# A new order of the transfer queue around the softmax shifts, an earlier first shift, and ten matmuls without use

## The chip, the cores and the metric

The kernel runs on one core of one Trainium2 chip. The metric is the device time of one execution in microseconds (us), as the median of several runs. The engines are TensorE (PE in the profile, its weight loads PEld), VectorE (DVE), ScalarE (ACT), GpSimd (POOL) and SyncE (SP), which here only issues transfers (SPq).

## The reference

An x of 1024 tokens by 256 features goes through four residual steps. The changed code lies in the first, attention over 16 heads of 16 with low-rank additions to its four weights:

```python
def lora_linear(x, W, b, Bm, Am):
    out = jnp.einsum('bld,od->blo', x, W) + b
    upd = jnp.einsum('blr,or->blo', jnp.einsum('bld,rd->blr', x, Bm), Am)
    return out + SCALING * upd
q = _split(lora_linear(x, Wq, bq, Bq, Aq))
k = _split(lora_linear(x, Wk, bk, Bk, Ak))
v = _split(lora_linear(x, Wv, bv, Bv, Av))
scores = jnp.einsum('bhqd,bhkd->bhqk', q, k) * SCALE
attn = jax.nn.softmax(scores, axis=-1)
out = jnp.einsum('bhqk,bhkd->bhqd', attn, v)
...
return lora_linear(out, Wo, bo, Bo, Ao)
...
x = x + _L0_attn_a_ref(_layernorm(x, axis=-1), ...)
x = x + _L0_ffn_ref(_layernorm(x, axis=-1), ...)
x = x + _L0_attn_b_ref(_layernorm(x, axis=-1), ...)
x = x + _L0_ffn_ref(_layernorm(x, axis=-1), ...)
```

## The kernel before

The program is written engine by engine; each engine runs its own list in the order of the code, and semaphores tie the lists together. There are three stages.

**Setup** (to about 52 us). Layer norm, transposes, and each weight merged with its low-rank part on PE (`merged_weight`, 4 identity products and 2 short ones, each fp32 product counted twice by the profile, into one bank of PSUM, then copied to `wT` by ACT). K and Q are projected and cut into a first fp16 part and a rest. For the scores each head needs its rows packed side by side, 64 rows of keys and of queries; that packing is done by transfers alone, most of them on SP's queue (`near_keys`, `queries`, `whole_group`). The heads form four groups of four (`G = 4`, `NG = 4`). Group 0 is packed head by head, group 1 right behind it; each whole group ends with two large transfers that repeat the rows on the other 64 partitions. A head of groups 2 and 3 takes 6 transfers of SP (two halves of rows, for the keys and for each half of the queries), so a group takes 24, and then the two repeats.

**Attention**, in eight units (a group and one half of the queries; `NU = 8`). A unit is done twice over, in two passes:
- The *max pass* finds each query's largest score: `max_tile` (PE, two matmuls side by side into a pair of banks, four pairs of products a head, 16 tiles a unit) and `take_max` (DVE, one reduction over 128x1024 a tile, `mx`). The banks alternate between two pairs, so tile k waits until DVE has taken tile k-2. After 16 tiles `cut_max` splits the 16 columns of maxima into two fp16 parts (`m_parts`). `shift_rows` turns them to rows on PE, `copy_shift` (ACT) takes them to `m_rows`, and `land_shift` (SP, 8 KB) writes them into rows of the packed queries. That subtraction, "the shift", then comes with the score product itself, so no score tile of the unit may start before its shift has landed (`shift_landed`).
- The *score pass*: `score_tile` (PE, one matmul, three banks in a ring), exp (ACT), and `times_v` (PE, 4 fp32 products, counted as 8, for every 4 score tiles, summed in bank 6, `PV_BANK`), 8 of these a unit.

PE runs the score pass of unit u beside the max pass of unit u+1 in one written order, `unit`. A unit's max pass is ahead: its first 7 tiles (`LEAD`) are done in the last part of the unit before. The shift of unit u+1 is turned at step 23 of unit u (`SHIFT_AT`) and is waited for at step 32, the first score tile of unit u+1. Ahead of unit 0 there is a lead of its own, in straight code: 7 max tiles of unit 1, and among them the sums of the feed-forward weights, the merge of Wo (used only after attention), the first shift, and the first three score tiles.

SP's list around it: group 1, the shift of unit 0, group 2 whole, two bias loads to be used after attention, the shift of unit 1, group 3 whole, the shift of unit 2, and the other five shifts. ACT waits for the packing of groups 2 and 3 at the end of its units 0 and 1 together, PE for group 2 at that place and for group 3 two units later.

**The tail** (from about 207 us): the last unit's scores beside everything else, in an order written out as one table of events for all engines. The change touches nothing there.

Names for PSUM banks: `drained5` counts how often bank 5 has been read out, `filled5` how often it was filled.

## Time and profile before

| | us |
|---|---|
| median of 3 runs | 353.88 |
| lowest, highest | 352.8, 354.6 |
| the profiled execution | 356.42 |
| its span, first to last instruction | 354.6 |
| mean granted clock of TensorE in it | 0.966 |
| PE busy | 327.8 (92%) |
| DVE busy | 280.8 (79%) |
| ACT busy | 243.6 (69%) |
| POOL busy | 128.5 (36%) |

All times below are read from the profiled execution and count from the start of its span. "Busy" is the time in which an engine worked on an instruction; of PE it says less than of the others, since matmuls overlap. "Granted clock" is the share of TensorE's full 2.4 GHz; it has two levels here, 1.00 and 0.50 (1.2 GHz).

### The profile page before, as it was taken

The page shows a single profiled execution, that of the slowest core. Times are in us where ns is not written, and L with a number is a line of the kernel's source. Part 1 is how long each engine was busy: PE and PEld are TensorE (multiplying, and loading weights), DVE is VectorE, ACT ScalarE, POOL GpSimd, SP SyncE. Part 2 cuts the span into 40 slices and gives each one's busy share as a digit, 9 for nine tenths or more (in the row PEclk, how much of TensorE's full clock was granted, in tenths as well). Part 3 has the DMA queues.
Part 4 walks back from the last instruction along what each step waited for, and adds up shares of the span by engine and source line. Part 5 has one row for each costly group of instructions (what it writes and reads, how often), then busy time and mean ns, then how long its engine had stood idle before and what let it go on. Part 6 is the DMA issues. An engine that isn't in the chain of part 4 may idle for free.

```text
span 354.6 us, 5515 instructions
## 1 busy us (share of the span) xinstructions
PE 327.8 (92%) x1909; PEld 146.6 (41%) x1909; DVE 280.8 (79%) x471; ACT 243.6 (69%) x465; POOL 128.5 (36%) x133
## 2 busy tenths in 40 slices
PE   7999787999979999999999999999998979789796
PEld 2653342222212222222222235339645736347585
DVE  6456999899968999999999443527869987989764
ACT  1575113688958898988889866896579333577694
POOL 5042018999200000000005001300599949995030
PEclk9999998799989999999999999999999969989899
DMA  7927861354340000000000000000000000000011
GB/s 214 321 58 122 146 181 30 71 115 85 63 91 0 3 0 1 2 0 3 0 3 1 3 1 2 0 0 2 0 3 0 1 0 2 0 0 2 1 61 59
DMA packets 14814, 14.57 MB, mean 41 GB/s; under 512 B 4995, under 2 KB 13126, under 8 KB 14598
## 3 DMA queue, kind: packets, MB, share of 16 engines
q1 hardware_dynamic: 12358, 12.09, 15.1%
q10 hardware_dynamic: 2176, 1.64, 1.5%
q0 software_dynamic: 256, 0.52, 0.8%
q8 instruction: 15, 0.25, 0.3%
q14 instruction: 9, 0.07, 0.1%
HBM read 5.78 MB, written 1.05 MB: 19 GB/s over the span
## 4 chain that ended last, share of the span: by engine, by line
PE 61%; SPq 10%; DVE 8%; ACT 7%; POOL 5%; DMA 4%; issue 3%; ACTq 0%; DVEq 0%; POOLq 0%
PE ps L1419 14%; PE ps L1405 12%; SPq L535 8%; PE ps L1547 6%; PE ps L1559 6%; PE ps L1382 5%; DVE mx L1097 3%; POOL pbuf L750 3%; PE ps L1334 3%; PE ps L1532 3%; PE ps L1591 2%; PE ps L1364 2%; DMA parts<-pbuf 1%; DMA pack<-m_rows 1%; ACT ps L931 1%
## 5 line engine op out<-in xcount | busy, mean ns | idle before, releaser
L1097 DVE TENSOR_REDUCE mx<-ps 128x1 f32<-128x1024 f32 x128 | 150.4, 1219 | 10.2 <-PE ps L1382 9.0
L888 ACT ACTIVATE pbuf<-ps 128x512 f32<-128x512 f32 x256 | 135.8, 601 | 29.7 <-PE ps L1405 28.5
L1405 PE MATMUL ps<-pack 64*128 64x512 f16 x256 | 87.9, 387 | 3.7 <-DMA pack<-m_rows 1.9
L1419 PE MATMUL ps<-pbuf,v_slot 128*32 128x512 f32 x512 | 69.7, 618 | 1.2 <-ACT parts L873 1.2
L1405 PEld LDWEIGHTS ps<-pack 64*128 64x128 f16 x256 | 23.1, 94 | 82.2 <-ACT pbuf L888 49.3
L1382 PE MATMUL ps<-pack 64*128 64x512 f16 x128 | 49.2, 387 | 5.1 <-DVE mx L1097 4.2
L750 POOL TENSOR_TENSOR pbuf<-wT 128x1024 f32<-128x1024 f32 (+3 forms) x32 | 48.3, 1550 | 4.7 <-ACT wT L960 4.7
L1382 PE MATMUL ps<-parts,pack 64*128 64x512 f16 x128 | 50.0, 396 | 0.0
L705 POOL COPY v_slot<-v_sb 128x512 f32<-128x512 f32 x8 | 4.8, 612 | 114.2 <-PE ps L1419 92.2
L681 POOL TENSOR_TENSOR rstd<-rstd,minus_half 128x2 f32<-128x2 f32 x16 | 11.4, 715 | 72.4 <-DVE rstd L1016 72.4
L1191 DVE SCALAR_TENSOR_TENSOR pack<-ps,g_unit,pack 128x512 f16<-128x512 f32 (+1 forms) x40 | 24.7, 640 | 15.2 <-ACT pack L943 15.1
L1547 PE MATMUL ps<-v_sb,w_nat 128*128 128x512 f16 (+1 forms) x160 | 32.8, 351 | 2.4 <-DVE v_sb L1183 2.4
L1559 PE MATMUL ps<-w_nat,pack 128*128 128x256 bf16 x256 | 31.4, 273 | 0.2 <-DVE pack L1191 0.2
L931 ACT ACTIVATE ps<-ps,b_col 128x512 f32<-128x512 f32 (+1 forms) x40 | 23.4, 610 | 8.9 <-PE ps L1547 8.9
L1204 DVE TENSOR_REDUCE s_wide<-pbuf 128x64 f32<-128x1024 f32 (+3 forms) x32 | 25.4, 813 | 2.2 <-POOL pbuf L750 2.1
L1559 PEld LDWEIGHTS ps<-w_nat,pack 128*128 128x128 f16 x256 | 25.0, 98 | 4.9 <-issue 0.6
L943 ACT ACTIVATE pack<-ps,g_unit 128x512 f16<-128x512 f32 (+1 forms) x40 | 23.5, 642 | 0.2
L953 ACT ACTIVATE xn<-x_res,offset,rstd 128x256 f32<-128x256 f32 x24 | 13.1, 595 | 14.6 <-POOL offset L686 14.5
L1547 PEld LDWEIGHTS ps<-v_sb,w_nat 128*128 128x128 f16 x160 | 15.8, 102 | 16.4 <-issue 3.6
L1382 PEld LDWEIGHTS ps<-pack 64*128 64x128 f16 x128 | 11.9, 94 | 23.4 <-DVE mx L1097 12.3
L1419 PEld LDWEIGHTS ps<-pbuf,v_slot 128*32 128x32 f32 x512 | 10.5, 108 | 18.9 <-issue 18.2
L1591 PE MATMUL ps<-w_nat,xT 128*128 128x512 f32 x32 | 17.2, 664 | 0.0
(145 smaller groups left out, 392.0 us busy)
## 6 DMA issues: line engine op xcount, KB each, us to landing
w_nat<-in_L_ffn_w_dram SPq DMA_DIRECT2D x2, 1024.0 KB, 6.7
pack<-pack SPq DMA_DIRECT2D x3, 512.0 KB, 4.9
pack<-pbuf SPq DMA_DIRECT2D x20, 64.0 KB, 3.0
x_res<-in_L_attn_a_x_dram SPq DMA_DIRECT2D x4, 256.0 KB, 3.9
pack<-parts SPq DMA_DIRECT2D x16, 64.0 KB, 2.3
pack<-parts SPq DMA_DIRECT2D x32, 32.0 KB, 2.0
out_dram<-x_res SPq DMA_DIRECT2D x4, 256.0 KB, 2.1
w_nat<-in_L_attn_b_Wqkv_dram ACTq DMA_DIRECT2D x1, 768.0 KB, 4.8
```

What stands on the lines that cost most here:

```text
L535: eng.dma_start(rows[ROWS // 2 * i:ROWS // 2 * i + ROWS // 2], terms).then_inc(done, 16)
L750: pool.tensor_tensor(out, in0, in1, ALU.mult).then_inc(products, 1)
L888: act.activation(pbuf[:, c % 2, j, :], ps[:, b, :], ACT.Exp, scale=scale_reg).then_inc(drained[b], 1)
L931: act.activation(src, src, ACT.Gelu, bias=b1_col[:, f:f + 1]).then_inc(gelu_ready, 1)
L1097: dve.tensor_reduce(mx[:, par, k:k + 1], ps[:, b:b + 2, :].rearrange("p b k -> p (b k)"), AX_X, ALU.max) \
L1191: dve.scalar_tensor_tensor(out=g_lo[:, kept(r, s), f, 0:width], in0=bank(key)[:, 0:width], scalar=g_unit[:, f:f + 1], in1=g_hi[:, kept(r, ...
L1204: dve.tensor_reduce(s_raw[:, t % 2, i, 0:nj], terms, AX_X, ALU.add).then_inc(reduced, 1)
L1382: ins = pe.matmul(ps[:, b + n, :], q.rearrange("p g t -> p (g t)"), keys.rearrange("p g t -> p (g t)"), start=True, stop=True)
L1405: pe.matmul(ps[:, b, :], k_group[0:ROWS, at, j, P * c:P * c + P].rearrange("p g t -> p (g t)"), q_rows[0:ROWS, at, qh, j, :].rearrange("p ...
L1419: ins = pe.matmul(ps[32 * j:32 * j + 32, PV_BANK, :], v_slot[:, qh, c, j, :], pbuf[:, c % 2, j, :], start=(c == 0), stop=(c == TT - 1))
L1547: ins = pe.matmul(out, w1T[:, c, P * f:P * f + P], x12[:, part, c, v], start=(part == 0 and c == 0), stop=(part == 1 and c == DC - 1))
L1559: ins = pe.matmul(out, part[:, k, f, v], w2T[:, f, :], start=(f == 0 and n == 0 and i == 0), stop=(f == FC - 1 and n == 1 and i == 1))
```

## The change

Three edits, of which none changes what is computed.

1. On PE, in the lead: the weight sums stay behind max tile 0; the first shift's transpose and Wo's merge move from behind tile 0 to behind tile 1, in the opposite order. Their two banks are swapped with that (shift 5, merge 7). ACT copies the shift ahead of Wo's merged weight.
2. On PE, behind each of the lead's tiles 2 to 6: two matmuls of 128x512 bf16 on constants into bank 6, whose result is overwritten (`KEEP_UP = 2`).
3. On SP: the first head of group 2 ahead of the first shift, the other three behind it; the second shift behind group 2's repeats and ahead of the bias loads; the third shift behind three of group 3's heads, and the fourth head and the repeats behind that.

```diff
@@ setup order
-    return [("proj", 6), ("proj", 7), *(("v", t) for t in range(TT)), ("wsum",), ("wt", O_), ("shift",)]
+    return [("proj", 6), ("proj", 7), *(("v", t) for t in range(TT)), ("wsum",), ("shift",), ("wt", O_)]
@@ SP
+            sp.wait_ge(rest_ready, len(ITEMS))
+            pack_heads(2, 0, 1)
             land_shift(0, 0, 0)
-            sp.wait_ge(rest_ready, len(ITEMS))
+            pack_heads(2, 1, G - 1)
             sp.wait_ge(abs_ready, 2)
-            whole_group(2)
+            repeat_group(2)
+            land_shift(0, 1, 1)
             is_drained(sp, ("wt", O_))
             for tile, name in ((b2_all, "L0_ffn_b2"), (bout_all, "L0_attn_b_bout")):
                 sp.dma_start(tile, a[name].unsqueeze(0).broadcast_to([P, D])).then_inc(later_bias_in, 16)
-            land_shift(0, 1, 1)
-            whole_group(3)
+            pack_heads(3, 0, G - 1)
             land_shift(1, 0, 2)
+            pack_heads(3, G - 1, 1)
+            repeat_group(3)
@@ ACT
-            evacuate_weight(O_)
-            act.wait_ge(cols_in, 16)
...
             copy_shift(0)
+            evacuate_weight(O_)
+            act.wait_ge(cols_in, 16)
@@ PE
-            def keep_clock(n):
+            def keep_clock(n, b):
                 for _ in range(n):
-                    pe.matmul(ps[:, PAIR_BANKS[0], :], onesb[:, 0:P], onesb[:, :], start=True, stop=True)
+                    pe.matmul(ps[:, b, :], onesb[:, 0:P], onesb[:, :], start=True, stop=True)
...
             for k in range(LEAD):
                 max_tile(0, 1, 1, k)
                 if k == 0:
+                    weight_sums(("wsum",))
+                if k == 1:
                     pe.wait_ge(consts, 6)
-                    weight_sums(("wsum",))
+                    shift_rows(0)
                     merged_weight(("wt", O_))
-                    shift_rows(0)
+                    is_drained(pe, ("v", TT - 1))
+                if k >= LEAD - 5:
+                    keep_clock(KEEP_UP, PV_BANK)
                 if k == LEAD - 4:
                     pe.wait_ge(far_keys_packed, 16 * G)
                     pe.wait_ge(shift_landed, 16)
```

`pack_heads(g, first, n)` issues the packing transfers of n heads, `repeat_group(g)` waits for the group's packing and issues the two repeats; together they are the old `whole_group`.

PE's list in the lead, before: `abs_sum` is the weight sums, the four rows behind it are the merge and the shift's transpose, `pack`/`parts,pack` pairs are max tiles, a single `pack` is a score tile.

```order
L1358 MATMUL ps<-abs_sum,ones 128x2 [waits drained4,abs_ready,consts]
L1296 MATMUL ps<-ident,w_nat 128x128 [waits drained5,w_in3]
L1296 MATMUL ps<-ident,w_nat 128x128 x3
L1302 MATMUL ps<-aT,b_all 128x256 x2
L1396 MATMUL ps<-identh,m_parts 128x128 [waits drained7,shift_split]
L1382 MATMUL ps<-pack 128x512 [waits drained2]
L1382 MATMUL ps<-parts,pack 128x512
L1382 MATMUL ps<-pack 128x512 [waits drained0]
L1382 MATMUL ps<-parts,pack 128x512
L1382 MATMUL ps<-pack 128x512 [waits drained2]
L1382 MATMUL ps<-parts,pack 128x512
L1405 MATMUL ps<-pack 128x512 [waits drained4,shift_landed,far_keys_packed]
```

And now:

```order
L1390 MATMUL ps<-pack 128x512 [waits drained2]
L1390 MATMUL ps<-parts,pack 128x512
L1404 MATMUL ps<-identh,m_parts 128x128 [waits drained5,shift_split,consts]
L1304 MATMUL ps<-ident,w_nat 128x128 [waits drained7,w_in3]
L1304 MATMUL ps<-ident,w_nat 128x128 x3
L1310 MATMUL ps<-aT,b_all 128x256 x2
L1390 MATMUL ps<-pack 128x512 [waits drained0,drained6]
L1390 MATMUL ps<-parts,pack 128x512
L1372 MATMUL ps<-onesb 128x512 x2
L1390 MATMUL ps<-pack 128x512 [waits drained2]
L1390 MATMUL ps<-parts,pack 128x512
L1372 MATMUL ps<-onesb 128x512 x2
```

Max tile 1 and the shift's transpose stand ahead of the merge, and pairs of constant matmuls (`onesb`) stand between the tiles.

SP's list from group 1's repeats on, before (`pack<-parts` is the packing of group 2 or 3, `pack<-m_rows` a shift):

```order
L615 DMA pack<-pack 64x4096
L629 DMA pack<-m_rows 2x16x128 [waits drained7]
L535 DMA pack<-parts 32x1x1024 [waits abs_ready,rest_ready]
L535 DMA pack<-parts 32x1x1024
L535 DMA pack<-parts 32x1x512 x4
L535 DMA pack<-parts 32x1x1024 x2
...
L613 DMA parts<-pack 64x4x512 [waits group_packed2]
L615 DMA pack<-pack 64x4096
L638 DMA w_nat<-in_L_ffn_b_dram 128x256 [waits drained5]
L638 DMA w_nat<-in_L_attn_b_bout_dram 128x256
L629 DMA pack<-m_rows 2x16x128 [waits drained7]
L535 DMA pack<-parts 32x1x1024 x2
```

And now:

```order
L536 DMA pack<-parts 32x1x1024 [waits rest_ready]
L536 DMA pack<-parts 32x1x1024
L536 DMA pack<-parts 32x1x512 x4
L633 DMA pack<-m_rows 2x16x128 [waits drained5]
L536 DMA pack<-parts 32x1x1024 x2
L536 DMA pack<-parts 32x1x512 x4
...
L616 DMA parts<-pack 64x4x512 [waits group_packed2,abs_ready]
L618 DMA pack<-pack 64x4096
L633 DMA pack<-m_rows 2x16x128 [waits drained7]
L645 DMA w_nat<-in_L_ffn_b_dram 128x256 [waits drained7]
L645 DMA w_nat<-in_L_attn_b_bout_dram 128x256
```

One head's six transfers moved ahead of the first shift, and the second shift moved ahead of the two bias loads. The end of SP's list for the attention, now:

```order
L536 DMA pack<-parts 32x1x1024 x2
L536 DMA pack<-parts 32x1x512 x4
L633 DMA pack<-m_rows 2x16x128 [waits drained7]
L536 DMA pack<-parts 32x1x1024 x2
L536 DMA pack<-parts 32x1x512 x4
L616 DMA parts<-pack 64x4x512 [waits group_packed3]
L618 DMA pack<-pack 64x4096
L633 DMA pack<-m_rows 2x16x128 [waits drained7] x5
```

The third shift, which stood behind both repeats of group 3, stands ahead of its last head.

## Rows read from the trace of the kernel before

**Rows 1.** The page, 40 equal slices of the span: TensorE's granted clock, in tenths.

```profile
PEclk9999998799989999999999999999999969989899
```

**Rows 2.** Stretches: length; busy us (instructions) of PE, PEld, DVE, ACT, POOL; clock, DMA share, GB/s.

```profile
57.00:59.00 2.00, 0.95 (x6) 0.39 (x7) 2.00 (x3) 0.84 (x2) 1.84 (x2) 0.98 0.45 74
59.00:61.00 2.00, 1.89 (x6) 0.21 (x3) 2.00 (x3) 0.84 (x2) 1.91 (x2) 0.50 0.18 37
...
101.00:103.00 2.00, 0.10 (x3) 0.06 (x3) 1.27 (x2) 0.46 (x1) 0.00 (x0) 1.00 0.55 115
...
105.00:107.00 2.00, 2.00 (x13) 0.29 (x6) 0.37 (x1) 0.25 (x2) 0.51 (x1) 0.58 0.00 0
```

**Rows 3.** PE's timeline in the lead: start, us, line, operation, count, idle before and releaser.

```profile
52.59 1.14 PE L1296 MATMUL ps<-ident,w_nat 128*128 128x128 f32 x8
54.71 0.23 PE L1396 MATMUL ps<-identh,m_parts 128*128 128x128 f16 x1
54.88 0.39 PE L1382 MATMUL ps<-pack 64*128 64x512 f16 x1
...
57.66 0.37 PE L1405 MATMUL ps<-pack 64*128 64x512 f16 x1 [0.68 <-issue]
...
63.35 1.93 PE L1419 MATMUL ps<-pbuf,v_slot 128*32 128x512 f32 x8
...
66.85 1.07 PE L1419 MATMUL ps<-pbuf,v_slot 128*32 128x512 f32 x8
```

**Rows 4.** DVE's timeline over the same stretch.

```profile
53.32 0.18 DVE L1106 SCALAR_TENSOR_TENSOR m_parts<-mx,m_parts 128x16 f16<-128x16 f32 x1
...
55.31 9.14 DVE L1097 TENSOR_REDUCE mx<-ps 128x1 f32<-128x1024 f32 x8 [0.55 <-PE ps L1382]
66.10 8.40 DVE L1097 TENSOR_REDUCE mx<-ps 128x1 f32<-128x1024 f32 x7 [1.65 <-PE ps L1382]
```

**Rows 5.** The timeline of SP's transfer queue: when each was issued, and how long issuing took.

```profile
48.09 0.62 SPq L615 DMA_DIRECT2D pack<-pack  x1
55.60 0.78 SPq L629 DMA_DIRECT2D pack<-m_rows  x1
56.51 16.70 SPq L535 DMA_DIRECT2D pack<-parts  x24
...
76.71 2.04 SPq L638 DMA_DIRECT2D w_nat<-in_L_attn_b_bout_dram  x1
78.80 0.73 SPq L629 DMA_DIRECT2D pack<-m_rows  x1
79.58 16.16 SPq L535 DMA_DIRECT2D pack<-parts  x24
...
97.85 0.61 SPq L615 DMA_DIRECT2D pack<-pack  x1
98.51 0.72 SPq L629 DMA_DIRECT2D pack<-m_rows  x1
```

**Rows 6.** PE's and PEld's timeline at the first score tile of units 1 and 2.

```profile
81.15 0.11 PEld L1405 LDWEIGHTS ps<-pack 64*128 64x128 f16 x2 [0.46 <-DMA pack<-m_rows]
...
102.94 0.39 PE L1405 MATMUL ps<-pack 64*128 64x512 f16 x1 [1.90 <-DMA pack<-m_rows]
```

**Rows 7.** The shifts of units 1 to 4 turned on PE, from the timeline.

```profile
75.50 0.23 PE L1396 MATMUL ps<-identh,m_parts 128*128 128x128 f16 x1 [0.41 <-DVE m_parts L1106]
...
95.36 0.23 PE L1396 MATMUL ps<-identh,m_parts 128*128 128x128 f16 x1
...
118.73 0.23 PE L1396 MATMUL ps<-identh,m_parts 128*128 128x128 f16 x1
...
138.44 0.23 PE L1396 MATMUL ps<-identh,m_parts 128*128 128x128 f16 x1
```

**Rows 8.** Timeline behind unit 3's shift: its issue by SP; ACT's copy of unit 2's output.

```profile
119.29 0.66 SPq L629 DMA_DIRECT2D pack<-m_rows  x1
...
127.12 0.58 ACT L873 COPY parts<-ps 128x512 f32 x1
```

More of the change, by code:

```diff
@@ L73 @@
 WARM_UP = 17
+KEEP_UP = 2
 SCORE_BANKS = (4, 5, 7)
@@ L605, in _, with pack_heads @@
             sp.dma_start(q_rows[ROWS:2 * ROWS, 0, 1, :, :], q_rows[0:ROWS, 0, 1, :, :]).then_inc(second_half_repeated, 16)
-            def whole_group(g):
-                for h in range(G * g, G * g + G):
+            def pack_heads(g, first, n):
+                for h in range(G * g + first, G * g + first + n):
                     near_keys(sp, h, whole, group_packed[g])
@@ L611, in whole_group, with repeat_group @@
                         queries(sp, h, 0, qh, group_packed[g])
+            def repeat_group(g):
                 sp.wait_ge(group_packed[g], group_count(g))
@@ L616, in whole_group @@
                              q_rows[0:ROWS, g, :, :, :].rearrange("p s j t -> p (s j t)")).then_inc(group_repeated[g], 16)
-            whole_group(1)
+            pack_heads(1, 0, G)
+            repeat_group(1)
             def land_shift(g, qh, u):
@@ L1361, in _ @@
                      "v": project_v, "wsum": weight_sums, "norm2": norm_squared}
-            def keep_clock(n):
+            def keep_clock(n, b):
                 for _ in range(n):
-                    pe.matmul(ps[:, PAIR_BANKS[0], :], onesb[:, 0:P], onesb[:, :], start=True, stop=True)
+                    pe.matmul(ps[:, b, :], onesb[:, 0:P], onesb[:, :], start=True, stop=True)
             pe.wait_ge(consts, 4)
-            keep_clock(WARM_UP)
+            keep_clock(WARM_UP, PAIR_BANKS[0])
             for key in setup_order():
```

## The prediction

> **What bounds the kernel now.** First the page's slices [rows 1]: TensorE's clock is below full in slices 7 and 8 (53 to 71 us), in slice 12 (98 to 106 us) and in three slices of the tail. The change touches the first two places. The stretches narrow them down [rows 2]: the clock is 0.50 from 59 to 61 us (it fell at 58.9), PE did 0.10 us of work from 101 to 103, and behind that the clock is down again, from 103.2 until past 106. Nowhere else between 60 and 200 us is PE idle for long. So in the regular part PE sets the pace, and there is a ruler for it: the shifts, turned once a unit [rows 7], at 75.50, 95.36, 118.73 and 138.44. The last interval is 19.71 us and has neither an idle PE nor a low clock in it. The one before is 23.37, the one before that 19.86. What exceeds 19.71 is what the places of the second kind cost in all, wait and clock together: 3.66 and 0.15 us.
>
> Then the reasons. At 102.94 PE had waited 1.90 us for a transfer `pack<-m_rows` [rows 6], the shift of unit 2. ACT had its rows ready at about 95.9 (unit 3's shift, met by an idle SP, is issued 0.56 us behind its transpose [rows 7, 8]; for unit 2 that is 95.92). SP issued it at 98.51 [rows 5], because it stood behind group 3's last packing, its landing and both repeats; and it landed 4.4 us after its issue, since 768 KB of repeats were on the way, where the first shift took 2.06 (55.60 to the score at 57.66) [rows 3, 5]. The shift of unit 1 likewise: ready at 76.1, issued at 78.80 behind the bias loads, waited for 0.46 us at 81.15 [rows 5, 6].
>
> In the lead DVE is the bound: eight reductions follow each other from 55.31 to 64.45, 1.13 us from one to the next, and beside one of them PE has a max tile and at most one score tile, 512 columns each, 0.21 us at 2.4 GHz. PE works 0.95 of 2 us from 57 to 59 [rows 2], and the clock falls. The price shows later: the first `times_v` takes 1.93 instead of 1.07 [rows 3], so max tile 9 comes late, and DVE stands idle 1.65 us before 66.10 [rows 4].
>
> **Part 1: the shift of unit 2 goes ahead of group 3's last head.** Its place in SP's list is now behind 18 packing transfers instead of 24, a landing and two repeats. SP's time: bias loads end at about 77 (below), 18 transfers at 16.16/24 = 0.67 us [rows 5] take 12.1, so SP is free at 89 to 90 and waits for ACT. The shift is issued on time and lands 2.1 to 2.4 us later, with nothing large in flight. PE asks for it 5.7 us behind the transpose (101.04 against 95.36). The slack is 5.7 - 0.56 - 2.4 = 2.7 us. The wait of 1.90 goes, and with it the idle stretch behind which the clock fell. Together **3.66 us**, by the ruler. If only the wait went and the clock fell all the same, it would be 1.90; nothing in the intervals from 118 on, where PE is equally busy, gives a reason for a fall.
>
> The SP list pays for it with 6 transfers and the repeats that now stand behind the shift. Who waits: ACT wants group 3's packing at the end of unit 1, right behind its copy of that unit's output. The regular distance from transpose to that copy is 127.12 - 118.73 = 8.39 us, and the copy lasts 0.58. From the transpose to the last head's landing: 0.56 + 0.73 for the shift + 6 x 0.67 + 2.1 for a landing (unit 0's shift [rows 3, 5]) = 7.4 us [rows 5, 8]. Slack 1.6 us, with the copy's time, so it costs nothing; it is thin, and is a rival below. PE wants the repeats of group 3 only two units later.
>
> **Part 2: the shift of unit 1 goes ahead of the bias loads.** Group 2's packing starts a head earlier (SP was idle from 48.71 to 55.60 [rows 5]; six transfers of 0.67 to 0.70 fill 4.2 us of that). The other 18 go out from 54.9 to 67.4, land at 69.5, and the repeats are out by 71, landed by about 76. The shift of unit 1 is ready near 74.1 (76.1 less part 3's gain), so SP is free for it. Even if the repeats hold it up as unit 2's was held, 5.0 us from the repeat's issue to the landing, it is there at 76.5, and PE asks at about 79. Gain **0.15 us** by the ruler. The bias loads (2.75 us of issuing) are wanted after attention only.
>
> **Part 3: the lead.** The maxima are cut at 53.50 [rows 4]. The transpose now stands behind max tile 1 (which starts as DVE frees its bank, at 53.0) and runs at about 53.6; ACT is idle, so SP issues at about 54.1 instead of 55.60, and the shift lands at 56.2 instead of 57.66. The merge takes 54.71 - 52.59 = 2.12 us [rows 3] wherever it stands: now 53.8 to 55.9, and max tile 2 behind it. DVE has tiles 0 and 1 to do meanwhile (53.55 to 55.83) and gets tile 2 at 56.3; before, it began tile 2 at 56.45. So **0.1 us** for DVE's queue. The earlier landing is no gain on its own, but PE now fills the gaps in which it waited.
>
> The matmuls without use: 0.21 us each at full clock, a pair 0.43. Beside a tile and a score tile this makes 0.86 us in DVE's 1.13, so ten of them cost nothing while the clock is up, and PE is at work for three quarters of 56 to 61 us where it was for less than half (0.95 of 2 us [rows 2]). Bank 6 is free by then. If the clock stays up, DVE's chain has no hole at its ninth tile: reductions end at 64.3 and go on. On PE, first `times_v` at 62.5 to 63.5, max tile 10 as soon as DVE frees its bank at 64.3, second `times_v` at 64.9 instead of 66.85 [rows 3]. From here PE is the bound, one `times_v` every 2.39 us. **1.9 us** (the 0.1 in it). Bounds for the clock's share: 0 if it falls all the same, 1.95 if it stays. I take the upper end: the row behind which the clock fell has PE at work for 48% of the time, and with the pairs it is 76%.
>
> A page of the Trainium skill says the same in principle: "TensorE: Matmul & The Clock Gate", section "What's actually happening", the throttled state is the default and activity releases it. The same page, section "Part 4: PE-mode transpose", says that transposes do not count as the engine being busy. The merge is made of products with an identity; if these went uncounted too, the clock would fall ahead of the lead's tiles. That is rival D. Here the trace speaks against it: the merge ran from 52.59 to 54.71 [rows 3], and the clock stayed up for 4 us more.
>
> **Sum**: 3.66 + 0.15 + 1.95 = 5.8 us (rounded), nothing added on the path. Against the profiled execution 356.42 - 5.8 = 350.6. That execution is 2.5 us above the median of the runs, which lie within 1.8 us of each other; the same 5.8 off the median gives 348.1. The tail starts earlier as a whole and keeps its order. Its three low-clock stretches can come out differently by a microsecond or two either way; I have no sign for that and put it in the range.
>
> **Rivals.**
> - *B, the clock falls in the lead anyway*, at about the same place. For: PE's gaps of 0.3 us behind each tile stay. Then the second cost of a fall remains (1.85 of 1.95 is not gained), and at 1.2 GHz tile, pair and score take 0.43 + 0.86 + 0.43 = 1.72 us against DVE's 1.13, so the two tiles left after 58.9 lose 0.6 each: 348.1 + 1.85 + 1.2 = **351.1**.
> - *C, ACT's wait for group 3 becomes the new stall*. If the last head lands like unit 2's shift did (4.4 us instead of 2.0) and one issue stalls by 1 us, as the mean of 0.70 in the first group hides, ACT waits 3.4 - 1.6 = 1.8 us, and the clock falls behind it as at 103.2 (3.66 - 1.90 = 1.8): **351.7**. Against: the last six transfers have the queue for themselves.
> - *D, the clock falls ahead of the lead's tiles*, at 53 to 55 us, behind PE's waits for DVE near the end of unit 0's max pass. From that point the edit works against itself: merge 2.1 us longer, five tiles at 1.72 instead of 1.13 (+3.0), the first `times_v` 0.9, scores and tiles beside it 0.6: 348.1 + 6.6 = **354.7**, slower than before. It decides from a fall before about 55 us on.
> - *F, the timed runs do not have the second fall.* The profiled run is 2.5 us above the median; if that is because others lose no clock behind the wait, only 1.90 of 3.66 is there to be gained: **349.9**.
> - *The change doesn't do what it says*: SP's order does not bring unit 2's shift in time. That would leave 353.88 - 2.1 = 351.8. Against it stand 2.7 us of slack.
>
> **How the numbers follow.** Forecast 348.1: 0.55. F 0.16, B 0.12, C 0.06, no effect of SP's order 0.03, D 0.05, anything else slower 0.03. The range reaches from 346.6 (the forecast less the runs' own spread) to 351.3, which takes in F and B and leaves out about 2 in 10. About 0.5% is what a measurement of this kernel can tell from no change: below 352.1 is faster, above 355.6 slower. The forecast, F, nearly all of B and most of C and of the case without effect are faster: 0.88. D's middle lies within 0.5%: 0.08 with the upper ends of B and C. Slower 0.04.
>
> **What the changed profile would show.** Right: granted clock 1.00 from 53 to 106 us; DVE without a hole over 0.5 us between 56 and 75; the transposes near 53.6, 73.5, 93.3, 113.0, at intervals of 19.7; no wait of PE for `pack<-m_rows`; ACT's first exp near 57.6. Wrong: constant matmuls 0.43 us apart (B or D), ACT idle behind its copy of unit 1's output until `pack<-parts` lands (C), an interval of over 20 us between the second and third transposes after the first (unit 2's shift late). My number is wrong if the two places are mended and the tail is longer by as much.

## The result, and the profile after

| | before | after |
|---|---|---|
| median of runs, us | 354.24 (4 runs) | 350.34 (4 runs) |
| lowest, highest | 352.8, 354.82 | 348.84, 351.1 |
| the profiled execution | 356.42 | 350.39 |
| its span | 354.6 | 348.6 |

The ratio of after to before is 0.989, with a 95% interval of 0.9845 to 0.9936. A second measurement on another chip, with 12 runs of the changed kernel and 29 of the kernel before, gave medians of 349.51 and 353.16 and a ratio of 0.9935 (0.9899 to 0.9972). Medians here are over all executions, the ratios over those within 1.5% of the kernel's fastest, and the profiled execution of the kernel before (356.42) counts among the slow ones that are left out. So the change makes the kernel 3.7 to 3.9 us faster by the medians, and by the ratios 3.9 us in the first measurement and 2.3 (1.0 to 3.6) in the second. The forecast was 348.1, a gain of 5.8. Between the two profiled executions the gain is 6.0 us. The experiments had to explain why the profiles show 6 and the timed executions less than 4.

The page of the changed kernel, TensorE's granted clock in 40 slices, answers [rows 1]. Only the tail still has low slices:

```profile
PEclk9999999999999999999999999999999969889899
```

The stretches in which the kernel before had its low clock and its idle PE [rows 2]; the columns are the same:

```profile
57.00:59.00 2.00, 1.47 (x9) 0.32 (x8) 1.83 (x3) 0.60 (x1) 1.90 (x2) 1.00 0.40 63
59.00:61.00 2.00, 2.00 (x10) 0.37 (x10) 2.00 (x3) 1.18 (x2) 1.91 (x2) 1.00 0.29 62
...
101.00:103.00 2.00, 1.82 (x16) 0.53 (x13) 1.96 (x3) 1.84 (x4) 0.52 (x1) 1.00 0.83 184
103.00:105.00 2.00, 2.00 (x19) 0.67 (x16) 1.72 (x2) 1.92 (x5) 0.00 (x0) 1.00 0.99 209
```

PE is at work for 1.82 us of 101 to 103, where it had 0.10, and the clock is 1.00 throughout. PE's timeline in the lead, against [rows 3]; L1404 is the shift's transpose, L1304 the merge, L1372 the constant matmuls, L1413 a score tile, L1427 `times_v`:

```profile
53.31 0.22 PE L1404 MATMUL ps<-identh,m_parts 128*128 128x128 f16 x1
53.43 1.13 PE L1304 MATMUL ps<-ident,w_nat 128*128 128x128 f32 x8
...
55.87 0.60 PE L1372 MATMUL ps<-onesb 128*128 128x512 bf16 x2
...
57.87 0.37 PE L1413 MATMUL ps<-pack 64*128 64x512 f16 x1 [0.53 <-issue]
...
62.58 1.06 PE L1427 MATMUL ps<-pbuf,v_slot 128*32 128x512 f32 x8
...
64.97 1.06 PE L1427 MATMUL ps<-pbuf,v_slot 128*32 128x512 f32 x8
```

The first two `times_v` start at 62.58 and 64.97, where the forecast had 62.5 and 64.9. DVE, against [rows 4]:

```profile
53.03 0.18 DVE L1114 SCALAR_TENSOR_TENSOR m_parts<-mx,m_parts 128x16 f16<-128x16 f32 x1
...
55.98 2.36 DVE L1105 TENSOR_REDUCE mx<-ps 128x1 f32<-128x1024 f32 x2 [0.38 <-PE ps L1390]
58.50 14.13 DVE L1105 TENSOR_REDUCE mx<-ps 128x1 f32<-128x1024 f32 x12 [0.17 <-PE ps L1390]
```

The hole of 1.65 us behind the ninth tile is gone. SP's queue, against [rows 5]:

```profile
49.62 0.61 SPq L618 DMA_DIRECT2D pack<-pack  x1
50.28 5.53 SPq L536 DMA_DIRECT2D pack<-parts  x6
55.85 0.74 SPq L633 DMA_DIRECT2D pack<-m_rows  x1
56.64 11.83 SPq L536 DMA_DIRECT2D pack<-parts  x18
...
74.11 0.72 SPq L633 DMA_DIRECT2D pack<-m_rows  x1
...
93.83 0.69 SPq L633 DMA_DIRECT2D pack<-m_rows  x1
94.55 4.34 SPq L536 DMA_DIRECT2D pack<-parts  x6
100.31 0.65 SPq L616 DMA_DIRECT2D parts<-pack  x1
```

The second and third shift are issued 0.55 and 0.56 us behind their transposes, which PE's timeline has at:

```profile
73.56 0.23 PE L1404 MATMUL ps<-identh,m_parts 128*128 128x128 f16 x1 [0.34 <-DVE m_parts L1114]
...
93.27 0.23 PE L1404 MATMUL ps<-identh,m_parts 128*128 128x128 f16 x1
...
112.98 0.23 PE L1404 MATMUL ps<-identh,m_parts 128*128 128x128 f16 x1
```

The intervals between transposes are 19.71 us from the second on, as in the undisturbed part of [rows 7]. From the cut of unit 0's maxima to the fourth transpose the kernel before takes 118.73 - 53.32 = 65.41 us and this one 112.98 - 53.03 = 59.95.

### The profile page after: what moved, and what is told of

It is laid out like the page before. It is cut to its first block, busy times and chain, and to the rows that moved or that the text cites. A ratio compares the mean times of both kernels' runs of the same rounds, so it can differ in the third digit from the quotient of the medians.

```text
span 348.6 us, 5536 instructions
## 1 busy us (share of the span) xinstructions
PE 326.4 (94%) x1919; PEld 147.5 (42%) x1919; DVE 280.8 (81%) x471; ACT 243.4 (70%) x465; POOL 128.6 (37%) x133
## 4 chain that ended last, share of the span: by engine, by line
PE 75%; DVE 9%; ACT 7%; POOL 5%; issue 3%; ACTq 0%; DVEq 0%; POOLq 0%
PE ps L1427 18%; PE ps L1413 16%; PE ps L1390 7%; PE ps L1559 6%; PE ps L1571 6%; PE ps L1342 4%; DVE mx L1105 4%; POOL pbuf L758 3%; PE ps L1544 3%; PE ps L1372 3%; PE ps L1603 2%; ACT ps L939 1%; PE ps L1331 1%; PE ps L1310 1%; ACT parts L879 1%
## 5 line engine op out<-in xcount | busy, mean ns | idle before, releaser
L1413 PE MATMUL ps<-pack 64*128 64x512 f16 x256 | 85.9, 379 | 1.6 <-ACT pbuf L894 1.0
L1427 PE MATMUL ps<-pbuf,v_slot 128*32 128x512 f32 x512 | 68.0, 604 | 1.2 <-ACT parts L879 1.2
L1413 PEld LDWEIGHTS ps<-pack 64*128 64x128 f16 x256 | 23.0, 93 | 79.1 <-ACT pbuf L894 49.7
L1390 PE MATMUL ps<-pack 64*128 64x512 f16 x128 | 48.1, 378 | 3.3 <-DVE mx L1105 3.1
L1390 PE MATMUL ps<-parts,pack 64*128 64x512 f16 x128 | 49.2, 386 | 0.0
L961 ACT ACTIVATE xn<-x_res,offset,rstd 128x256 f32<-128x256 f32 x24 | 13.1, 595 | 14.6 <-POOL offset L694 14.5
L1427 PEld LDWEIGHTS ps<-pbuf,v_slot 128*32 128x32 f32 x512 | 10.4, 107 | 17.6 <-issue 16.9
```

Of the source, the lines that this page charges most:

```text
L1390: ins = pe.matmul(ps[:, b + n, :], q.rearrange("p g t -> p (g t)"), keys.rearrange("p g t -> p (g t)"), start=True, stop=True)
L1413: pe.matmul(ps[:, b, :], k_group[0:ROWS, at, j, P * c:P * c + P].rearrange("p g t -> p (g t)"), q_rows[0:ROWS, at, qh, j, :].rearrange("p ...
L1427: ins = pe.matmul(ps[32 * j:32 * j + 32, PV_BANK, :], v_slot[:, qh, c, j, :], pbuf[:, c % 2, j, :], start=(c == 0), stop=(c == TT - 1))
```

## The measure used in the experiments

Each profile is split at two points: the cut of unit 0's maxima on DVE ("cut") and the transpose of the shift of unit 3 on PE ("T4"). The stretch between them holds all that the change touches; what follows T4 is code that it leaves alone, except in experiment 8. T2 and T3 are the transposes of the shifts of units 1 and 2, and T1 that of unit 0. All in us. The last column is the ratio to the kernel before as measured beside it, with its 95% interval.

| kernel | cut to T2 | T2 to T3 | T3 to T4 | cut to T4 | T4 to the end | median of its runs | ratio to before |
|---|---|---|---|---|---|---|---|
| before, first profile | 22.18 | 19.86 | 23.37 | 65.41 | 235.9 | 354.24 | |
| before, second (experiment 1) | 21.51 | 20.71 | 21.78 | 64.00 | 232.3 | 352.67 | 1.0006 (0.9937 to 1.0075) |
| before, third (experiment 11) | 23.44 | 19.71 | 20.53 | 63.68 | 233.7 | 353.27 (18 runs) | |
| after, first profile | 20.53 | 19.71 | 19.71 | 59.95 | 235.6 | 350.34 | 0.9891 (0.9845 to 0.9936) |
| after, second (6) | 21.32 | 19.71 | 19.71 | 60.74 | 233.5 | 349.51 | 0.9935 (0.9899 to 0.9972) |
| after without constants (2) | 23.52 | 19.72 | 19.71 | 62.95 | 233.9 | 351.49 | 0.9966 (0.9903 to 1.0028) |
| before, SP's order new (3) | 22.19 | 19.72 | 19.70 | 61.61 | 233.9 | 350.57 | 0.9927 (0.9861 to 0.9992) |
| before, constants only (4) | 20.05 | 23.14 | 19.71 | 62.90 | 232.3 | 353.11 | 1.0004 (0.9939 to 1.0069) |
| after, SP's order old (5) | 19.88 | 21.09 | 22.90 | 63.87 | 233.9 | 350.85 | 0.9942 (0.9910 to 0.9974) |
| four more constants (7) | 19.89 | 19.71 | 19.71 | 59.31 | 235.8 | 349.15 | 0.9889 (0.9842 to 0.9936) |
| the same again (12) | 19.89 | 19.71 | 19.71 | 59.31 | 233.8 | 348.25 | 0.9895 (0.9835 to 0.9956) |
| constants in the tail (8) | 19.89 | 19.71 | 19.71 | 59.31 | 235.8 | 351.92 | 0.9947 (0.9912 to 0.9983) |
| after, PE's order old (9) | 20.05 | 19.71 | 19.71 | 59.47 | 232.2 | 347.96 | 0.9893 (0.9839 to 0.9948) |
| four more constants, shift first (10) | 19.88 | 20.04 | 19.71 | 59.63 | 233.9 | 349.29 | 0.9901 (0.9863 to 0.9939) |

The unchanged last stretch differs by up to 3.7 us between single executions, and it goes with the time that TensorE spends at the low clock in it: under 4 us in the three profiles at 232.2 and 232.3, about 7 us in the seven at 233.5 to 233.9, 14 to 17 us in the three at 235.6 to 235.9 (experiment 8 is the exception, see there). That is why a step is judged here by its own stretch and only the whole by medians. Experiments 1 to 4 ran on one chip, 5 to 8 on a second, 9 to 12 on a third; the kernel before had medians of 354.56, 353.16 and 353.27 there.

## Experiments 1 and 11: the kernel before, again

The edit is none. Two theories for the missing 2 us:

> The kernel before once more, unchanged, for a second profile of it. The change moved the profiled execution by 6.0 us (356.42 to 350.39) but the medians by only 3.9 (354.24 to 350.34). Theory F: other executions of the kernel before lose less behind the wait for unit 2's shift, because the clock does not fall there: the interval between the third and fourth transpose of a shift is then about 21.6 us (19.71 plus the 1.9 of waiting) instead of 23.37, and the profiled execution near 354.3. Theory G: the attention costs the same as in the first profile (intervals 19.86 and 23.37) and the 2 us lie in the tail, from the last shift's transpose (197.6) to the end of the span, 157.0 us there: then that stretch is near 155.

> The kernel before, unchanged, for a third profile: from SP's issue of the first shift to PE's first matmul behind unit 2's shift 47.3 to 47.5 us again, whatever the clock did in the lead; the fourth transpose 65 to 67 us behind the lead's first max tile (66.7 if the clock falls behind the wait, 65.3 if not).

Theory F holds for the attention. PE's rows in the second profile: the wait for unit 2's shift, and the transposes around it.

```profile
94.53 0.23 PE L1396 MATMUL ps<-identh,m_parts 128*128 128x128 f16 x1
...
102.11 0.39 PE L1405 MATMUL ps<-pack 64*128 64x512 f16 x1 [1.90 <-DMA pack<-m_rows]
...
116.31 0.23 PE L1396 MATMUL ps<-identh,m_parts 128*128 128x128 f16 x1
```

The wait is 1.90 us as in the first profile, to the hundredth, but the clock does not fall behind it:

```profile
101.00:103.00 2.00, 0.89 (x5) 0.30 (x5) 0.51 (x2) 0.38 (x1) 0.00 (x0) 1.00 0.05 12
103.00:105.00 2.00, 2.00 (x16) 0.55 (x15) 1.48 (x2) 1.70 (x5) 0.61 (x1) 1.00 0.00 0
105.00:107.00 2.00, 1.83 (x14) 0.45 (x13) 2.00 (x2) 2.00 (x5) 0.00 (x0) 1.00 0.00 0
```

T3 to T4 is 21.78 instead of 23.37 (expected: 21.6). The same idle stretch can be followed by a low clock or not; what decides it, no run here shows. Theory G also has a share: the last stretch is 232.3 us here against 235.9, so the first profile was unlucky in the tail as well. Both add up to the whole difference between the two spans (6.0 = 1.4 + 3.6 + 1.0 of setup).

What stays the same in all profiles with SP's old order is something the forecast had not seen. SP's rows for the first shift, from the second and the third profile of before and from experiments 5 and 4:

```profile
54.63 0.78 SPq L629 DMA_DIRECT2D pack<-m_rows  x1
```

```profile
54.75 0.78 SPq L629 DMA_DIRECT2D pack<-m_rows  x1
```

```profile
54.39 0.78 SPq L630 DMA_DIRECT2D pack<-m_rows  x1
```

```profile
55.05 0.78 SPq L630 DMA_DIRECT2D pack<-m_rows  x1
```

And PE's first score tile behind unit 2's shift in the third profile of before and in experiment 5:

```profile
101.66 0.39 PE L1405 MATMUL ps<-pack 64*128 64x512 f16 x1 [0.65 <-DMA pack<-m_rows]
```

```profile
101.85 0.39 PE L1406 MATMUL ps<-pack 64*128 64x512 f16 x1 [1.62 <-DMA pack<-m_rows]
```

From SP's issue of the first shift to that score tile: 47.34 us in the first profile (55.60 to 102.94), 47.48 in the second, 46.91 in the third, 47.46 in experiment 5, and 46.28 in experiment 4, where only the tile's weight load waited, 0.19 us, until 101.33. The differences are those of the issuing itself: the 48 packing transfers of groups 2 and 3 take 32.86, 32.99, 32.39, 32.96 and 31.79 us to issue there, and what is left is 14.5 us in all five. PE's own pace up to there differs by more than 3 us (cut to T2 is 19.88 to 23.44), and its wait takes up the difference: 0.65 us where PE was late, 1.90 where it was early. So in the three profiles of before SP's list sets the time from the first shift to unit 2's, and what PE lost in the lead was not on the path. From that score tile to T4 it is 14.20 us in the second and third profile and 15.79 in the first, where the clock is low behind it.

The expectation said 47.3 to 47.5 and 65 to 67 us from the lead's first tile. The third profile's 46.91 is under that by 0.4, and its 64.98 from the lead's first tile just under 65; in the table's measure the three are at 65.41, 64.00 and 63.68.

## Experiment 3: SP's order alone

```diff
+            sp.wait_ge(rest_ready, len(ITEMS))
+            pack_heads(2, 0, 1)
             land_shift(0, 0, 0)
-            sp.wait_ge(rest_ready, len(ITEMS))
+            pack_heads(2, 1, G - 1)
             sp.wait_ge(abs_ready, 2)
-            whole_group(2)
+            repeat_group(2)
+            land_shift(0, 1, 1)
...
-            land_shift(0, 1, 1)
-            whole_group(3)
+            pack_heads(3, 0, G - 1)
             land_shift(1, 0, 2)
+            pack_heads(3, G - 1, 1)
+            repeat_group(3)
```

> The kernel before with SP's new order of transfers alone; PE's and ACT's lists as before. The forecast's step: unit 1's and unit 2's shifts are no longer waited for, the intervals between transposes are 19.71 from the second on, so 3.8 us less in attention (350.4 from 354.2) while the lead keeps its fall. Under theory F the wait alone goes in most executions: 1.9 to 2.1 us less, 352.2. A lead that suffers from the head in front of the first shift would show as a first score tile later than 57.7.

The intervals are 19.72 and 19.70: nobody waits for a shift any more. Cut to T4 is 61.61, which is 2.1 to 3.8 us less than in the three profiles of before, where the whole change takes 2.9 to 5.5 off. The median is 350.57 against 354.56, the ratio 0.9927 (0.9861 to 0.9992), which only just leaves out 1. The same edit with the constant matmuls in place is the step from experiment 4 to experiment 9: 62.90 to 59.47, and the ratio goes from 1.0004 to 0.9893. So SP's order is the larger part of the whole change. In the lead the clock falls as before, and now that costs time on the path: the first `times_v` is slow, and DVE waits for tile 9.

```profile
63.51 1.93 PE L1426 MATMUL ps<-pbuf,v_slot 128*32 128x512 f32 x8
```

```profile
66.45 2.35 DVE L1104 TENSOR_REDUCE mx<-ps 128x1 f32<-128x1024 f32 x2 [1.85 <-PE ps L1389]
```

## Experiments 4 and 5: the lead without SP's order

Experiment 4 is the kernel before with the constant matmuls alone.

```diff
                     shift_rows(0)
+                    is_drained(pe, ("v", TT - 1))
+                if k >= LEAD - 5:
+                    keep_clock(KEEP_UP, PV_BANK)
                 if k == LEAD - 4:
```

> The kernel before with the ten matmuls on constants alone; lists otherwise as before. The forecast's step: clock stays at 1.00 through the lead, second transpose at about 73.7 instead of 75.50, the third interval keeps its wait for unit 2's shift and may grow: SP packs at its own pace (its issues bound it), so unit 2's shift is issued at 98.5 whatever PE does, and 1.8 us gained in the lead turn into 1.8 us more of waiting there. If so the median is that of the kernel before, 354.2 within 0.5. Rival: PE's gain carries through, 352.4.

The lead is repaired: DVE reduces 15 tiles in a row, and T2 comes 20.05 us behind the cut.

```profile
54.76 17.52 DVE L1098 TENSOR_REDUCE mx<-ps 128x1 f32<-128x1024 f32 x15 [0.55 <-PE ps L1383]
```

Then PE is too early for SP, at the first score tile of unit 1:

```profile
80.12 0.52 PE L1406 MATMUL ps<-pack 64*128 64x512 f16 x1 [1.62 <-DMA pack<-m_rows]
```

```profile
80.00:82.00 2.00, 1.88 (x9) 0.55 (x13) 0.46 (x1) 1.13 (x3) 1.90 (x2) 0.56 0.44 77
```

The wait came at unit 1's shift, not at unit 2's as expected, with a fall of the clock behind it; T2 to T3 is 23.14. Unit 2's shift is issued at 96.90 and not at 98.5: the first shift went out 0.55 us earlier than in the first profile, and the packing behind it 1.07 us faster, for which no run shows a cause. Against the second and third profile of before 1.5 and 3.4 us are gained to T2, but only 1.1 and 0.8 are left at T4. That is no more than unit 2's shift came earlier behind the cut, 48.56 us instead of 49.80 and 49.48. (Against the first profile 2.1 and 2.5 us are gained, since that one lost 1.5 us more to the clock behind its wait.) What PE gained in the lead is given back. The median is 353.11 and the ratio 1.0004 (0.9939 to 1.0069), no difference that can be told.

Experiment 5 is the changed kernel with SP's old list (the diff of experiment 3 in reverse).

> The changed kernel with SP's order of before; PE's and ACT's lists and the ten constant matmuls as changed. Theory (two paces): SP's old list takes a fixed 47.5 us from the issue of the first shift to the landing of unit 2's shift (54.63 to 102.11, 55.05 to about 101 in the two profiles of before's SP order), whatever PE does. The new PE order brings the first shift 1.1 us earlier, so SP's pace gains that at most; from the lead's first max tile to the fourth transpose it takes 63 to 64 us (61.25 in the changed kernel, 66.71 and 65.30 in the two profiles of before). Rival (the gains add up one by one): the lead's 1.9 us come through, 61.25 + 3.8 = 65.1 with waits of 0.5 and 1.9 us. Median 1.5 to 2.5 us above the changed kernel.

Cut to T4 is 63.87. From the lead's first tile it is 65.17, nearer to the rival's 65.1 than to the theory's 63 to 64; but 54.39 to 101.85 is SP's 47.46, as the theory has it. The theory had left out that the clock can fall behind the wait, and here it did: PE waits 1.62 us and T3 to T4 is 22.90, where the second profile of before has 21.78 with a longer wait and no fall. Without these 1.6 us it would be 63.6. PE waits 1.21 us for unit 1's shift and 1.62 for unit 2's.

The expected 1.5 to 2.5 us above the changed kernel came out as 1.3 by the medians, and the ratios, 0.9942 and 0.9935, don't tell the two apart. But the ratio does tell this kernel from the one before: with SP's list as it was, PE's new order and the constants gain something together. In the profile the first shift is issued 0.82 us behind the cut, where it was 2.28 to 2.57 in the three of before, so SP's 47 us start 1.5 us earlier.

## Experiments 2 and 6: do the constant matmuls hold the clock?

```diff
-KEEP_UP = 2
+KEEP_UP = 0
```

> The changed kernel without the ten matmuls on constants (KEEP_UP = 0); everything else as changed. If they hold the clock up: it falls to 0.50 near 59 to 62 us as in the kernel before, DVE gets a hole of 1 to 2 us behind its ninth tile, the second transpose comes 1.5 to 2 us later than in the changed kernel (73.56), and the median is near 352.1. If the order of PE's list alone does it (the merge next to the lead's tiles fills the gaps), nothing falls and the median is that of the changed kernel, 350.3.

> The changed kernel once more, for a second profile and six more times beside the kernel before. If the ten matmuls hold the clock in every execution, the lead has clock 1.00 again and the fourth transpose comes 61.2 us behind the lead's first max tile. If the first profile was luck of where the clock falls (in e2 and in the second profile of before it fell at 53 to 54.5, ahead of the place where the constant matmuls stand), it falls at 53 to 55 here too and that stretch is 63 to 66 us. Ratio to before 0.989 by the first comparison, with an interval of 0.5% either side.

Expected was a fall at 59 to 62 us and a second transpose 1.5 to 2 us later. Without them the clock is at 0.50 from 54.4 to 67.6 us, DVE has holes of 2.19 and 1.80 us in the lead, and T2 comes 23.52 us behind the cut instead of 20.53:

```profile
58.24 8.01 DVE L1105 TENSOR_REDUCE mx<-ps 128x1 f32<-128x1024 f32 x7 [2.19 <-PE ps L1390]
68.05 8.40 DVE L1105 TENSOR_REDUCE mx<-ps 128x1 f32<-128x1024 f32 x7 [1.80 <-PE ps L1390]
```

The median is 351.49, and the ratio of 0.9966 (0.9903 to 1.0028) is told apart neither from the kernel before nor from the changed one. With them the second profile of the changed kernel has a fall too, at 55 us, just ahead of the first constant matmuls, but a short one:

```profile
54.00:55.00 1.00, 1.00 (x5) 0.66 (x4) 1.00 (x1) 0.00 (x0) 0.91 (x2) 1.00 0.27 50
55.00:56.00 1.00, 0.69 (x3) 0.23 (x4) 0.40 (x2) 0.59 (x1) 1.00 (x1) 0.50 0.23 39
...
59.00:60.00 1.00, 1.00 (x6) 0.22 (x5) 1.00 (x1) 0.62 (x2) 0.91 (x2) 1.00 0.18 41
```

It is over before the first `times_v`. Cut to T4 is 60.74, which is 0.8 us over the first profile and 1.4 over the 59.31 of the undisturbed ones. Of the 1.4, 1.1 is in DVE's reductions; the rest is an instruction of the next cut that takes 0.49 instead of 0.17 us (see the first shift, below).

Over all 14 profiles: the clock fell in the lead in each of the five without constant matmuls (three of before, experiments 2 and 3), in one of the six with ten and in none of the three with fourteen. The place matters, though. The second and third profile of before and experiment 2 have their fall at 53.2 to 54.2 us, ahead of the place of the first constant matmul (54.9 to 56.6), so the ten can't be what keeps such a fall away: one of six against three of five may be chance. The first profile of before and experiment 3 fell at 58.9 and 59.7, where the constants do stand, and none of the eight profiles with constants that came that far at full clock did. For this later fall the constants are the cause, as far as so few profiles can show it.

## Experiments 7, 12 and 10: four more, and the first shift first

Experiments 7 and 12 are one kernel, run twice.

```diff
             assert not side
+            is_drained(pe, ("v", TT - 1))
+            keep_clock(3, PV_BANK)
...
                     weight_sums(("wsum",))
+                    keep_clock(1, PV_BANK)
```

> The changed kernel with four more matmuls on constants: three between unit 0's last max tile and the lead's first, where PE stands idle 0.92 us, and one behind the first, where it stands idle 0.34. If falls at 53 to 55 us come from this idle stretch, there are none here, and the median is up to 1 us under the changed kernel where that loses some; if the changed kernel has no such falls, the two are equal within 0.2 us. Should the four delay the lead's first tiles, DVE's hole behind them grows from 0.38 us.

> The kernel with four earlier constant matmuls once more, to see whether it is better than the changed kernel: the clock 1.00 from 49 to 107 us again, interval 19.61 between the first two transposes, median 3.5 to 4.5 us under the kernel before. If its first profile was luck, the clock falls at 53 to 59 us here.

Both profiles have clock 1.00 from 49 to 107 us and the same 59.31 us from cut to T4; the hole behind the first tiles stays 0.38 us:

```profile
55.39 16.39 DVE L1105 TENSOR_REDUCE mx<-ps 128x1 f32<-128x1024 f32 x14 [0.38 <-PE ps L1390]
```

The medians, 349.15 (changed kernel on the same chip: 349.51) and 348.25, have ratios to before of 0.9889 (0.9842 to 0.9936) and 0.9895 (0.9835 to 0.9956). That is 0.6 us less in its stretch than the first profile of the changed kernel, and not told apart from it by the medians. The four more don't account for the 0.6 either: experiment 8, whose lead is the changed kernel's, has the same 59.31.

Experiment 10 puts the first shift ahead of the head again:

```diff
-            pack_heads(2, 0, 1)
             land_shift(0, 0, 0)
-            pack_heads(2, 1, G - 1)
+            pack_heads(2, 0, G)
```

> The kernel with four earlier constant matmuls (e7) with the first shift ahead of group 2's first head on SP again; otherwise the same. Theory: the head's six issues take 5.5 us when the queue is still full of group 1's repeats, and hold the first shift up to 55.85 in the changed kernel's profile, where PE then waits for it until 57.87 and the second transpose comes 20.25 us behind the first instead of 19.6. Then with the shift first its issue is 0.6 us behind its transpose, PE never waits for it, the interval is 19.6, and the median is equal to or up to 0.5 us under e7's (349.15). Cost: six issues later, group 3's last head lands 0 to 4 us later; if ACT then waits for it at about 101.7, an interval grows by 1 us or more.

The first shift is issued at 54.22, 0.62 us behind its transpose, and cut to T2 is 19.88. The price is where the forecast had looked for slack, one shift later: six more issues stand ahead of unit 1's shift, and PE waits for it,

```profile
79.05 0.39 PE L1412 MATMUL ps<-pack 64*128 64x512 f16 x1 [0.15 <-DMA pack<-m_rows]
```

which makes T2 to T3 20.04. No gain: 59.63 against 59.31, median 349.29.

## Experiment 9: PE's and ACT's old order with the rest

PE's list in the lead is that of before with constants, as in experiment 4; SP's order is the new one.

> The changed kernel with PE's and ACT's order of before (merge of Wo and the first shift behind the lead's first tile, merge first); SP's new order and the ten constant matmuls as changed. The forecast gave the reorder 0.1 us of its own. In the profiles with the old PE order and the clock up in the lead (the one with constant matmuls alone) the lead's first max tile to the second shift's transpose took 21.35 us, in those with the new order and the clock up 21.18 to 21.83. So: 21.2 to 21.8 here, intervals of 19.71 behind it, first max tile to fourth transpose near 60.8, median that of the changed kernel within 0.5 us. If the reorder matters (PE idles 1.1 us between the lead's tiles 2 and 3 in the old order), the clock falls at 57 to 60 us and the median is 0.5 to 1.5 us above the changed kernel.

The expected 21.2 to 21.8 from the lead's first tile to T2 came out as 21.35 (51.56 to 72.91), with T2 20.05 us behind the cut against 19.88 to 19.89 with the new order and no disturbance. So the earlier shift is worth 0.17 us at most, and a profile with PE's gap of 0.57 us

```profile
56.13 0.39 PE L1390 MATMUL ps<-pack 64*128 64x512 f16 x1 [0.57 <-DVE mx L1105]
```

did not lose the clock. Its median, 347.96, with a ratio of 0.9893 (0.9839 to 0.9948), is the lowest of all. It is not told apart from the changed kernel (0.989 and 0.9935) nor from experiment 12 on the same chip (348.25), and in its profile the tail is at the low clock for under 4 us. So the new order on PE and ACT has no gain of its own that shows beside SP's new order and the constants.

## Experiment 8: constants in the tail

```diff
+KEEP_TAIL = {("lnt", 2, 2): 6, ("bo_y", 2): 5, ("o", "b", 4): 4, ("h", 1, 0, 0): 5}
...
+                if e in KEEP_TAIL:
+                    to_fill(pe, e)
+                    keep_clock(KEEP_TAIL[e], uses[e][0])
                 if e[0] in TAIL_FILLS:
                     tail[e[0]](e)
```

> The changed kernel with 20 more matmuls on constants in the tail, into banks that are about to be filled, at four places where PE waited 1.2 to 1.8 us (279, 287, 300 and 305 us). Span behind the fourth transpose is 235.6 us in the changed kernel's profile and 232.3 to 235.9 in the others; the difference goes with the falls of the clock in it. If those four waits bring the falls on, the stretch is near 232 and the median 2 to 3 us lower (347.5). If PE's lower clock there costs nothing (VectorE and GpSimd bound that stretch), the falls go and the time stays. Up to 20 x 0.21 = 4 us could be lost where PE does not wait.

The page's clock line shows one low place in the tail, where the changed kernel had three:

```profile
PEclk9999999999999999999999999999999996999999
```

But that is not the constants' doing: the second profile of the changed kernel has one low place in the tail too, without them, and takes 233.5 us. The last stretch of experiment 8 takes 235.8. It is the exception named above: the low clock lasts about 7 us in it, as in the seven profiles with 233.5 to 233.9, and it is some 2 us longer. The median, 351.92, is 2.4 us above the changed kernel on the same chip, while the ratios (0.9947 and 0.9935) don't tell them apart. Some of the twenty run while PE has work: a group of five takes 1.86 us at 292, with PE at work right before and behind it and the clock low.

```profile
292.26 1.86 PE L1373 MATMUL ps<-onesb 128*128 128x512 bf16 x5
```

In this profile they cost 2 us and give nothing back that shows. Which of the four places costs it was not tried.

## Why the forecast was right in kind and too large in size

**The unit 2 step: the mechanism was right, its term was mis-sized.** The wait went, all of it, and unit 2's shift was issued 0.56 us behind its transpose as reckoned. But the term was 3.66 us, and 1.6 to 1.8 of it was a fall of the clock that stood in the one profile at hand. Of three profiles of before only that one has it. The other two show 2.07 and 0.82 us over 19.71. The text took the whole 5.8 off the median all the same, although the profiled execution stood 2.5 us above it. It had this as rival F, with 349.9 and a chance of 0.16; 350.34 is that case, and it lies in the range because the range was drawn to take F in. These 1.8 us are nearly all of the difference between 5.8 and 3.9.

**The lead's 1.95 us and the waits' 3.81 were added, but in the kernel before they are not two costs.** This is the step whose mechanism was wrong. The forecast took PE for the bound throughout and priced the lead by DVE's hole. In fact SP's 47 us from the first shift to unit 2's ran beside it and ended later. Experiment 4 shows it: the lead is repaired, 1.5 to 3.4 us are gained to T2, and at T4 no more is left than SP's list was quicker by (against the profiles without a fall behind the wait). For the whole change it made no difference to the sum: the intervals over 19.71 and the lead's gain make up cut to T4 by the way they are measured (65.41 - 59.95 = 5.46 in the first profiles, of the lead 1.65), whoever holds PE up. It would have misled about each edit alone. What the change can take from an execution without the fall is what SP's pace stands above PE's, 64.0 and 63.7 against 59.95 and 60.74: 2.9 to 4.1 us. The 3.7 to 3.9 of the medians lies in it, and the 2.3 (1.0 to 3.6) by the second ratio overlaps it. SP stood in the chain that ended last, with 8% of the span on its packing line; that row was on the page and was not used.

**The unit 1 step** had 0.15 us. It is 1.00 in the second profile of before and 0 in the third: it depends on how early PE comes, as the wait for unit 2 does. SP served the shift at once, 2.8 us behind the last repeat's issue.

**The first shift.** Forecast: issued at 54.1, landed at 56.2. In the changed kernel's first profile it was issued at 55.85 and the first score tile ran at 57.87, behind 0.53 us of waiting. The six issues of the head moved ahead of it took 5.53 us, not 4.2. They take 5.5 in every profile with this order, right behind group 1's repeats, and 3.8 to 4.9 for the last head of group 3, with nothing large in flight; that the repeats slow them is likely and was not tested apart. Cut to T2 became 20.53 instead of 19.89, a loss of 0.64 that the forecast had as nothing. Of it 0.26 is in DVE's reductions (with a hole of 0.17 us), and 0.38 is the first instruction of the next cut, which took 0.55 us instead of 0.17:

```profile
72.74 0.55 DVE L1112 TENSOR_SCALAR m_parts<-mx 128x16 f16<-128x16 f32 x1
```

That instruction is long in five of the 14 profiles (0.27 to 0.62 us), with and without the late shift, and no run shows why. In experiments 7, 8 and 12, where the first shift was issued 0.9 to 2.2 us behind its transpose and not 2.5, the same order lost nothing.

**The constant matmuls** did what was forecast, with no cost at full clock: the first `times_v` were foreseen to 0.1 us. Rival B (a fall at the same place) did not occur in nine profiles, rival D (a fall ahead of the tiles) in one. Its price was set far too high: 6.6 us against 0.8 to 1.4. The forecast let the low clock last through all five tiles, and it ended after the second.

**The group 3 step** (rival C): 7.04 us from the third transpose to the repeats' issue, where 7.4 was reckoned to the landing, and ACT's copy stood at 8.39 as it should. No wait.

**The tail.** "A microsecond or two either way" was the right caution: 232.2 to 235.9 us in kernels that share its code. Between the two first profiles the difference was small (235.9 and 235.6).

A figure of the Trainium skill bears on the landings: "DMA: Bandwidth & Descriptors", section "Anatomy of one DMA", gives a fixed part of about 2.0 us for one transfer (for transfers issued by GpSimd). The traces agree for SP's: 2.06 us from the first shift's issue to its use in [rows 3, 5].

## What to carry to other kernels

When PE is nearly always busy and still waits for a transfer now and then, follow the issuing queue from one such wait to the one before: if the time between two of its small, urgent transfers is the same whatever PE does, the queue is the path. What is gained on PE between the two then hardly shows (experiment 4); what starts the queue's stretch earlier can (experiment 5). Put urgent small transfers ahead of bulk packing and repeats, at the place in the list where the queue is free when they come due, and expect six issues to take longer than their count while large transfers are under way. And where the granted clock falls behind an idle stretch in one profile, price wait and clock apart, since the next execution may have the wait without the fall.

## What the runs showed of the hardware

- An equal wait of 1.90 us of PE was followed by a low clock in one execution of a kernel and by none in the next. Of the four waits of 1.62 to 1.90 us for a shift, three were followed by it.
- In the lead of the kernel before, the low clock lasted from 59 to 66 us in the first profile, from 53 to 64 in the second and from 53 to 67 in the third, and cut to T2 was 22.18, 21.51 and 23.44. The second is the shortest: most of its low clock lies where DVE sets the pace, and its first `times_v` took 1.62 us, against 1.93 in the other two.
- The time of the untouched last stretch went with its time at the low clock: 232.2 to 232.3 us with under 4 us of it, 235.6 to 235.9 with 14 to 17.
- With two matmuls of 128x512 bf16 on constants behind each of five tiles, a fall among these tiles, as in the two of five profiles without them that came there at full clock, was seen in none of eight. At full clock they had no cost that shows.
- Issuing six small transfers on SP took 5.5 us behind two large ones, and 3.8 to 4.9 us with nothing large in flight.
